# Attention with look-ahead scores and a gated feed-forward: heads taken in pairs, 64-row products in three passes, weights read transposed

## The reference

```python
xn = layernorm(x)                                  # x: 8 x 512 x 256
qu, ku, vu, qc, kc, vc = split(xn @ W_qkv.T)       # 8 heads of 64 each
term1     = where(causal, 0, (qc * s) @ vu.T)      # 512 x 512 per head
lookahead = where(causal, sigmoid((qu * s) @ ku.T), 0)
Su        = term1 @ lookahead.T
scores    = (qc * s) @ kc.T - silu(Su)
attn      = softmax(where(causal, -max, scores)) @ vc
h         = silu(xn @ w_gate.T) * (xn @ w_up.T)    # hidden 768, int weights / 127
out       = x + attn @ W_out.T + h @ w_down.T
```

## Time and profile before

| | |
|---|---|
| median of 3 runs | 1201.95 us |
| profiled execution, first to last instruction | 1197.5 us |
| PE, PEld busy | 1155.7 us (97%), 1049.7 us (88%) |
| DVE, ACT, POOL busy | 1046.0 us (87%), 924.4 us (77%), 543.8 us (45%) |
| prologue and first projections | to about 27 us |
| attention | about 27 to 1003 us |
| feed-forward and sum | 1003 to 1197.5 us |

### The profile page before, as it was taken

The page is one execution under the profiler, slowest core; times in us unless marked ns, Lnnn a source line. Parts: engine busy times, 40 slices in busy tenths (PEclk is TensorE's granted clock), DMA queues, the critical chain, the costliest instruction groups (busy, mean ns, idle before and its releaser), DMA issues. The chain is left out here.

```text
span 1197.5 us, 25023 instructions
## 1 busy us (share of the span) xinstructions
PE 1155.7 (97%) x7324; PEld 1049.7 (88%) x7324; DVE 1046.0 (87%) x2421; ACT 924.4 (77%) x2074; POOL 543.8 (45%) x915
## 2 busy tenths in 40 slices
PE   6999999999999999999999999999999987999997
PEld 5899898989898989898989898989899976999997
DVE  6799889989998999899989998999889987878885
ACT  5788888888888888888888888888888864434443
POOL 0455555546555555555655565556555550000000
PEclk9999999999999999999999999999999998999999
DMA  5111211121112111211121112111321112243332
GB/s 172 40 45 45 63 45 45 45 63 44 44 44 63 44 44 44 63 44 44 44 63 44 44 44 63 44 44 44 101 59 45 45 54 79 89 140 102 108 109 67
DMA packets 41491, 74.16 MB, mean 62 GB/s; under 512 B 3504, under 2 KB 24496, under 8 KB 41392
## 3 DMA queue, kind: packets, MB, share of 16 engines
q1 hardware_dynamic: 41392, 73.15, 21.2%
HBM read 27.00 MB, written 12.58 MB: 33 GB/s over the span
## 5 line engine op out<-in xcount | busy, mean ns | idle before, releaser
L719 PE MATMUL Su<-L_s,T_s 128*128 128x128 f32 (+3 forms) x1920 | 292.5, 299 | 1.8 <-POOL T_s L543 1.8
L719 PEld LDWEIGHTS Su<-L_s,T_s 128*128 128x128 f32 x1920 | 279.3, 190 | 16.4 <-POOL T_s L543 2.7
L553 POOL TENSOR_SCALAR prob<-prob,inv 128x512 f32<-128x512 f32 x252 | 274.5, 1096 | 13.1 <-DVE inv L1134 12.9
L638 PE MATMUL X<-xT,W 128*128 128x512 f32 x960 | 242.5, 394 | 3.0 <-PEq L130 3.0
L638 PEld LDWEIGHTS X<-xT,W 128*128 128x128 f32 x960 | 172.7, 189 | 33.6 <-issue 3.2
L527 POOL TENSOR_SCALAR_AFFINE_SELECT gate<-gate 128x128 f32<-128x128 f32 (+1 forms) x192 | 66.3, 346 | 262.3 <-DVE gate L1111 197.3
L899 ACT ACTIVATE gate<-Su 128x512 f32<-128x512 f32 (+1 forms) x192 | 101.4, 528 | 71.5 <-PE Su L719 70.4
L907 ACT ACTIVATE prob<-prob,least 128x512 f32<-128x512 f32 (+3 forms) x256 | 142.4, 561 | 7.6 <-DVE least L1122 7.2
L1111 DVE SCALAR_TENSOR_TENSOR gate<-gate,Su 128x512 f32<-128x512 f32 (+1 forms) x192 | 114.2, 595 | 27.3 <-ACT gate L899 17.4
L543 POOL TENSOR_SCALAR_AFFINE_SELECT T_s<-T_s 128x256 fp32r<-128x256 f32 x256 | 131.1, 542 | 13.3 <-DVE T_s L1103 9.2
L535 POOL TENSOR_SCALAR_AFFINE_SELECT tanh_l<-tanh_l 128x128 f32<-128x128 f32 (+1 forms) x192 | 62.6, 333 | 160.0 <-ACT tanh_l L875 157.8
(11 more groups left out here) (85 smaller groups left out, 2132.7 us busy)
## 6 DMA issues: line engine op xcount, KB each, us to landing
qu_s<-qu_s SPq DMA_DIRECT2D x64, 256.0 KB, 3.7
qc_s<-qc_s SPq DMA_DIRECT2D x64, 256.0 KB, 3.5
xb<-in_L_attn_x SPq DMA_DIRECT2D x16, 512.0 KB, 4.6
heads_out<-o_s SPq DMA_DIRECT2D x32, 256.0 KB, 2.0
f_o_in<-heads_out SPq DMA_DIRECT2D x8, 1024.0 KB, 5.7
f_xres<-in_L_attn_x SPq DMA_DIRECT2D x8, 512.0 KB, 4.6
out<-f_y SPq DMA_DIRECT2D x8, 512.0 KB, 3.2
w_raw<-in_L_attn_W_qkv SPq DMA_DIRECT2D x6, 512.0 KB, 7.4
```

Source lines behind the costliest of these rows:

```text
L553: last = pool.tensor_scalar(v, v, inv[:, hp, w - 1:w], None, ALU.mult)
L638: last = pe.matmul(bank[:, :], sh.W[:, a, k, cols], xT[:, c, k, :], start=(n == 0), stop=(n == 3 * KD - 1))
L719: last = pe.matmul(Su[slot][:, at:at + (J + 1) * P], T_s[:, hp, a, to:to + P], L_s[:, hp, c, WIDE[J + 1]:WIDE[J + 1] + (J + 1) * P], start ...
```

## The change

Attention now takes a pair of heads in a step, 32 steps instead of 64. The two heads' 64 numbers lie in partitions 0 to 63 and 64 to 127, as the projection leaves them; no operand is stored twice and SP's `dup` is gone. L, T and Sc are made in three passes (`PRODUCTS`) of 64-row matmuls, one for each head in turn, into two neighbouring banks. ACT, DVE and POOL then treat both heads in one instruction of 2 x 512 or 2 x 256 columns, except `minus_scores`, exp, reciprocal and `norm`, which stay single because each has a number per row and head. The eight banks are handed round by a table (`TURNS`), and every group of products waits for the groups that held its banks (`BEFORE`, `take_bank`). The tile that tanh writes is now the softmax's own (`tanh_l = prob`), so `minus_scores` of a pair waits until the next pair's look-ahead has been split. The order of a step is the new `step` of each engine. The weights come in transposed, so that the prologue's and the end's transposes of weights fall away, and a weight is split 1024 or 1536 columns at a time.

```diff
@@ prologue, build
-            for n in range(groups):
-                ...
-                for i in range(per):
-                    last = pe.transpose(banks[n % 6][:, i * P:(i + 1) * P],
-                                        raw[:, per * t + i, k * P:(k + 1) * P], sh.ident[:, :])
+                sp.dma_start(raw[:, :, t * INNER:(t + 1) * INNER],
+                             W_qkv[:, t * INNER:(t + 1) * INNER].rearrange("(k p) c -> p k c", p=P)) \
+                act.wait_ge(loaded[t], 16)
+                act.activation(sh.W[:, HIGH, :, cols], raw[:, :, cols], ACT.Copy,
-        a = np.ascontiguousarray(inputs[name])
+        a = np.ascontiguousarray(a if a.ndim == 3 else a.T)
@@ attention: banks
-X_BANKS = 4
+TURNS = [("L", 0, (0, 1)), ("L", 1, (2, 3)), ("L", 2, (4, 5)), ("T", 0, (6, 7)), ("T", 1, (0, 1)), ("T", 2, (2, 3)),
+         ("O", 0, (4, 5)), ("proj", QU, (6,)), ("proj", KU, (7,)), ("proj", VU, (0,)), ("V", 0, (1,)),
+         ("Sc", 0, (2, 3)), ("Sc", 1, (4, 5)), ("Sc", 2, (6, 7)), ("proj", QC, (0,)), ("proj", KC, (1,)),
+         ("XT", 0, (2, 3)), ("Su", 0, (4, 5)), ("Su", 1, (6, 7)), ("PT", 0, (0, 1)), ("PT", 1, (2,)),
+         ("PT", 2, (4, 5)), ("Su", 2, (6, 7))]
+        tanh_l = prob
@@ attention: products (the same in term1 and scores)
-                    for a in (HIGH, LOW):
-                        last = pe.matmul(bank[:, at:at + w * P], ku_s[:, s % 2, J * P:(J + 1) * P],
-                                         qu_s[:, s % 2, a, 0:w * P], start=(a == 0), stop=(a == 1))
+                    for n, (a, c) in enumerate(PRODUCTS):
+                        for h in range(2):
+                            rows = slice(h * DH, (h + 1) * DH)
+                            last = pe.matmul(both[:, h, at:at + w * P], ku_s[rows, a, J * P:(J + 1) * P],
+                                             qu_s[rows, c, 0:w * P], start=(n == 0), stop=(n == 2))
@@ attention: the order of PE
+            def step(part, b, q, g, back1, back2, ahead):
+                for j in range(3):
+                    look_ahead(part, b, g, j)
+                for j in range(3):
+                    term1(part, b, q, g, j)
+                if back2:
+                    attend(part, b, q, g)
+                if ahead:
+                    project(part, b, q, g, QU)
+                    project(part, b, q, g, KU)
+                    project(part, b, q, g, VU)
+                    values_into(take_bank(part, b, g, "V", 0), (q + 1) // 2 % 2, (q + 1) % 2)
+                if back1:
+                    for j in range(3):
+                        scores(part, b, q, g, j)
+                if ahead:
+                    project(part, b, q, g, QC)
+                    project(part, b, q, g, KC)
+                if q == 2:
+                    transpose_x(part, b, g)
+                sum_up(part, b, g, 0)
+                sum_up(part, b, g, 1)
+                if back1:
+                    turn_probs(part, b, g)
+                sum_up(part, b, g, 2)
@@ attention: ACT
-                act.activation(tanh_l[:, c:c + n], bank[:, 0:n], ACT.Tanh, scale=LOOK_SCALE).then_inc(tanh_done, 1)
+                act.activation(tanh_l[:, :, c:c + n], bank("L", j)[:, :, 0:n], ACT.Tanh, scale=LOOK_SCALE) \
+                   .then_inc(tanh_done, 1)
-                for h in range(2):
-                    last = act.activation(dst, bank[rows, :], ACT.Copy)
+                act.activation(dst, bank("proj", t)[:, :], ACT.Copy).then_inc(proj_high, 1)
@@ attention: DVE, the middle of a step
+                if back2:
+                    sum_o(g - 2, q % 2)
+                if ahead:
+                    low_proj(g + 1, QU, par)
+                    low_proj(g + 1, KU, par)
+                    low_proj(g + 1, VU, par)
+                    low_values(g + 2, (q + 1) // 2 % 2, (q + 1) % 2)
+                if back1:
+                    minus_scores(g - 1, 0)
+                    minus_scores(g - 1, 1)
+                    inverse(g - 1, 0)
+                    minus_scores(g - 1, 2)
@@ attention: SP
-                sp.dma_start(words[DH:P, 0, :, :], words[0:DH, 0, :, :]).then_inc(done, 16)
-                sp.dma_start(words[0:DH, 1, :, :], words[DH:P, 1, :, :]).then_inc(done, 16)
```

More of the change, by code:

```diff
@@ L699, in term1 @@
-                last.then_inc(filled, 1)
-            def scores(g, s, j):
-                hp, par, slot = s % 2, (s // 2) % 2, (s + j) % 2
-                if not (isinstance(g, int) and 3 * g + j < 2):
-                    pe.wait_ge(scores_emptied, 3 * g + j - 1)
+                    for n, (a, c) in enumerate(PRODUCTS):
+                        for h in range(2):
+                            rows = slice(h * DH, (h + 1) * DH)
+                            last = pe.matmul(both[:, h, at:at + w * P], vu_s[rows, a, J * P:(J + 1) * P],
+                                             qc_s[rows, q % 2, c, J * P:SEQ], start=(n == 0), stop=(n == 2))
@@ L831, in _ @@
-            for t in FIRST_PAIR:
-                project(FIRST, 0, -2, t, 0)
-            values(FIRST, 0, -2)
-            batches(pe, program)
-            finish(BATCH - 1)
+                    for n, (a, c) in enumerate(PRODUCTS):
+                        for h in range(2):
+                            rows = slice(h * DH, (h + 1) * DH)
+                            last = pe.matmul(both[:, h, at:at + w * P], qc_s[rows, par, a, I * P:(I + 1) * P],
+                                             kc_s[rows, par, c, 0:w * P], start=(n == 0), stop=(n == 2))
@@ new lines, in attend @@
+            def attend(part, b, q, g):
+                both = take_bank(part, b, g, "O", 0)
+                for h in range(2):
+                    slot = (2 * (q - 2) + h) % HEADS
+                    pe.wait_ge(PT_low, after(g - 2, 1 + h))
+                    for K in range(TT):
+                        at = WIDE[TT - K]
+                        for c in (HIGH, LOW):
+                            last = pe.matmul(both[:, h, K * P:SEQ], v_s[:, slot // 4, K, slot % 4, :, :],
+                                             PT_s[:, h, c, at:at + (TT - K) * P],
+                                             start=(K == 0 and c == HIGH), stop=(K == TT - 1 and c == LOW))
+                    last.then_inc(o_filled, 1)
@@ new lines, in _ @@
+            for t in PROJ_ORDER:
+                if t == QC:
+                    pe.wait_ge(proj_low, proj_count(0, VU))
+                if t == KC:
+                    pe.wait_ge(v_low, 1)
+                project_into(bank("proj", t)[:, :], t, 0)
+                if t == VU:
+                    values_into(bank("V", 0), 0, 0)
+            batches(pe, lambda b, part: run_steps(b, part, step))
+            attend(LAST, BATCH, 0, LAST_G + 1)
+            for j in range(3):
+                scores(LAST, BATCH, 0, LAST_G + 1, j)
@@ L917, in copy_o_low @@
[L917 to L935 removed]
+                    act.wait_ge(scores_emptied, after(g - 1, j))
@@ new lines, in gate_of, with exp_of @@
+                act.wait_ge(Su_filled, after(g, j))
+                act.activation(gate[:, :, c:c + n], bank("Su", j)[:, :, 0:n], ACT.Tanh, scale=SU_SCALE) \
+                   .then_inc(gate_done, 1)
+            def exp_of(g, j):
+                act.wait_ge(scores_emptied, after(g, j))
+                for h in range(2):
+                    for w in ROWS[j]:
+                        v = prob[:, h, WIDE[w]:WIDE[w] + w * P]
+                        last = act.activation(v, v, ACT.Exp, bias=least[:, h, w - 1:w], scale=-1.0,
+                                              accum_out=total[:, h, w - 1:w])
+                last.then_inc(exp_done, 1)
```

1236 lines of the change are left out of this document (451 added, 785 removed).

## The result

The kernel with the change takes **1366.9 us** (median of 4 runs, 1361.7 to 1368.6), where the kernel before took 1201.6 in the same rounds (1200.6 to 1202.2). The ratio is 1.137, interval 1.135 to 1.139. The forecast was 1274, range 1235 to 1345: the direction was right, but the loss is 165 us and not 72, and the time lies above the range.

The account below looks back on a forecast made before the run. It took PE's work to bound the kernel before, and a serial chain of 32.1 us a step after. Attention 47 us late plus 25 at the end gave 1270 us span, 1274 us with 4.5 for the median; range 1235 to 1345.

Parts of the forecast that it names:

- The ring: In each step, hand-overs through all engines from L's start to the next L; T at 4.9, scalings over at 28.6 us.
- the sum of a step: In attention, the serial chain of one step, L to next L, was put at 32.1 us, 2.1 more than before.
- PE's clock falls: Rival: a half-clock stretch follows each stall before T, 1.5 us x 30 steps = 45, giving 1319 us; chance 0.15.
- Su needs L and T split, which DVE has done near 12.6: Within a step, DVE's splits of L and T were to end 12.6 us after L starts, delaying nothing.
- The two ends: Before and after attention's middle: x first transposed at 102.7 us, 13 early; last transposes to feed-forward 74 us, 25 more.
- The estimate: At attention's end, the last pair was put at 35 us, 14 of them PT, its split, O, sum and store.
- The set of 64-row products: On PE, one pair's 64-row matmuls for L, T or Sc were put at 2.35 us, midway between 2.03 and 2.7.
- The bound of 2.7: On PE, a set takes 2.7 us if two half weight loads need 0.22 us one after the other.
- The halves take turns: Rival: the two heads' 64-row matmuls don't run together, a set is 4.05 us, the kernel 1364 us; chance 0.10.
- A switch drains PE: Rival: changing between 64 and 128 rows drains PE, at least 0.15 us each, +0.3 a step, 1283 us; chance 0.12.
- PE stays the bound: Rival: results come before PE asks, a step is PE's 27.6 to 28.5 us, the kernel 1147 or 1173; chance 0.08.
- the forecast's sum: PE's own work for a pair in attention was to become 28.5 us, 1.1 us less than before.

Follow-up runs that it names:

- edit 1: Against the changed kernel, ACT makes the gate of Su's third group ahead of the three tanh of L instead of behind them: 1266.4 us, ratio 1.056.
- 5: Against the changed kernel, ACT's gate goes ahead of L's tanh and POOL's masks of T wait for DVE's split of L: 1233.6 us, ratio 1.027.
- 6: On the kernel with gate first and masks late, DVE instead of POOL scales the middle group of four probabilities: 1201.9 us, ratio 1.001.
- Edit 2: Against the changed kernel, one wait more on POOL holds its masks of T until DVE has split L: 1346.7 us, ratio 1.123.
- Edit 8: On the kernel with gate first, masks late and DVE scaling, PE's batch loop turns before a batch's last PT, behind 48 queued matmuls: 1187.2 us, ratio 0.989.
- experiment 7: Against the changed kernel, both heads' L, T and Sc read partitions 0 to 63, so head 1's own are left out: 1620.9 us, one run.

## Why the forecast had the direction right and the size wrong

**The ring was right.** Of its steps, from L's start in the step at 540.23:

| | forecast | measured | from |
|---|---|---|---|
| T starts | 4.9 | 4.8 | 545.01 |
| values made | 15.3 | 15.2 | 555.40 |
| `minus_scores` begins | 16.7 | 17.4 | 557.66 |
| first scaling | 19.9 | 20.8 | 560.98 |
| scalings over, PT starts | 28.6 | 29.5 | 569.73 |

The times of `minus_scores` and of the first scaling come from DVE's and POOL's timelines of the kernel after:

```profile
553.84 1.39 DVE L911 TENSOR_TENSOR o_s<-X,o_low 64x512 f32<-64x512 f32 x2
...
557.66 0.68 DVE L879 CUSTOM_DVE_ANT_0 prob<-X,gate 128x512 f32<-128x512 f32 x1
```

```profile
560.98 8.52 POOL L457 TENSOR_SCALAR prob<-prob,inv 128x512 f32<-128x512 f32 x8 [7.61 <-DVE inv L891]
```

That this ring, and not PE, set the time is shown and not only read: edits 1, 5 and 6 each shorten one member of it, and take 100, 33 and 32 us off.

**The step that failed is the sum of a step, 32.1 us for 34.75.** 28 x 2.65 = 74 of the 93 us that were missed. It has three parts.

- *The clock, some 1.1 to 1.4 us.* "PE's clock falls" stood as a rival at 0.15 with 1.5 us a step. Its mechanism was right: T and O are 1.5 us longer in the step from 506.41 than in the next, and edit 1 took 1.5 us of busy time off PE beyond the stall. Its chance was wrong. The one argument against it was that PE is busy on both sides of the stall, and that held nothing up. It should have been a term of the chain. In the step from 506.41 it costs less than its 1.5: the values come 1.5 later than in the step at 540.23, but PT starts only 0.7 later (30.2 for 29.5), since at full clock the ring waits for DVE's queue there. In others it costs more: the step from 576.14, just behind a turn, takes 37.2 us, and in it T takes 3.89 us, O 3.95 and PT 4.07. The 1.1 to 1.4 are what is left once the other two parts are taken off; that is a difference, not a measurement.
- *DVE beside POOL, 1.0 us.* The ring at full clock is 29.5 + 2.15 + 1.5 = 33.2 us with PT and Su's last group, 1.1 over the forecast. "Su needs L and T split, which DVE has done near 12.6": it has them done at 553.84, 13.6 after L's start, and the O sum and the projections' low parts queue behind. The splits were priced by the earlier trace rows, where widths were scaled and neighbours were not. Edit 2 shows the neighbour's share.
- *The loop's turn, 0.2 to 0.5.* In the kernel after L starts at 438.28, 472.39, 506.41, 540.23 and 576.14: three steps of 33.8 to 34.1, and one of 35.9 at the turn. Of the 28 steps five hold a turn, 35.8 us in the mean, and the others 34.5. How much of that is the turn and how much the clock behind it no run separates: at 569.73 PT runs slowly too (3.75 us), in the turn before, at 432.51, it does not (2.40) and L waits 2.04. Edit 8 gave back 0.5 a pair. The forecast had no term for it.

**The two ends, +10 us each.** x was first turned at 112.5 where 102.7 was forecast. L of step 0 starts at 29.59 instead of 26.3: the first 18 projections take 5.93 us behind an idle PE, where they take 4.31 later on, and L waits 1.50 us for DVE's low parts with nothing else to do for PE. The first two steps are longer by the rest.

```profile
17.65 5.93 PE L513 MATMUL X<-xT,W 128*128 128x512 f32 x18 [6.55 <-PEq L126]
...
29.59 2.19 PE L543 MATMUL X<-qu_s,ku_s 64*128 64x512 f32 x24 [1.50 <-DVE kc_s L816]
```

From the last transposes of x to the feed-forward it was 84, not 74. The chain of the last pairs, beside the earlier trace rows:

```profile
1117.37 9.95 PE L588 MATMUL X<-L_s,T_s 128*128 128x512 f32 x48 [1.17 <-DVE least L879]
...
1136.84 4.47 PE L624 MATMUL X<-PT_s,v_s 128*128 128x512 f32 x16 [5.50 <-DVE PT_s L902]
...
1152.96 4.53 PE L597 MATMUL X<-ident,prob 128*128 128x128 f32 x20 [5.75 <-DVE prob L925]
1159.86 3.97 PE L624 MATMUL X<-PT_s,v_s 128*128 128x512 f32 x16 [2.37 <-DVE PT_s L902]
1170.05 2.06 PE L1124 MATMUL f_G<-xT,W 128*128 128x512 f32 x4 [6.22 <-issue]
```

PE waits 1.2 to 6.2 us ahead of each of these, and all but the last then run slowly: PT takes 4.5 us here and 2.4 in the middle, O 4.5 and 2.8, Su's first two groups 9.95 and 7.06. The estimate priced PE's part at full clock, at which they would be 8 us shorter ((9.95 - 7.06) + (4.47 - 2.77) + (4.53 - 2.40) + (3.97 - 2.77)). 74 + 10 + 10 makes 94, the miss.

**The set of 64-row products: 2.12 us, not 2.35.** The error is in the good direction, 0.4 us a step on the chain. The bound of 2.7 rested on two half loads that need 0.22 one after the other. The loads start 3 ns apart, as the matmuls do. By the Trainium skill, "TensorE: Matmul & The Clock Gate", section "Measured speedup vs the span model", the estimate was near 2.03, and the trace is closer to that page than to my middle.

**The other rivals.** *The halves take turns* gives 1364, and the kernel took 1366.9. It is refuted all the same: a set of 2.12 us, and the experiment with one half at 4.03. A time that fits says nothing about its cause. *A switch drains PE*: where no switch lies, a run ends 0.16 us after the next has started (547.12 + 2.77 against 549.73); at the switches, 64 to 128 rows and back, 0.07 after (545.01 + 2.18 against 547.12, 553.88 + 1.59 against 555.40). A switch thus costs 0.09 us, and the starts, which are not modelled as the ends are, say the same: 0.21 us from the last matmul of the values to the first of Sc, 0.12 from one matmul of the values to the next. For the switches out of a set this is inside the 2.12. The Trainium skill, "TensorEngine Tiling (Array Packing)", section "Key Properties", says that changing the tiling mode drains TensorE; the trace has a price for it, and four of them are under 0.4 us a step. *PE stays the bound*: that is what edit 8 comes near, 28.9 a pair, once both waits and most of the turn are gone; that kernel still has the longer end, 78.3 us from the last transposes of x to the feed-forward against 47.5.

**The prices of the edits.** The three that answer the ring (1, 5 and 6) add no work to PE: their gains are the ring's members, and the change loses by its order and not by its 64-row products. With that order mended a pair takes 28.88 us, 1.1 less than before. That is the figure of the forecast's sum, but by luck: with the set as measured the sum says 1.7, and what the turns of the loop still cost takes the difference. The kernel is 14 us faster than before.

## What to carry to other kernels

When heads or tiles are merged into one step, draw the ring of hand-overs through all engines before counting what each saves. A kernel whose steps overlap three ways hides hand-overs that a merged step puts in a row, and less work on every engine can make it slower. A stall of PE of a few microseconds that comes in every step is to be priced twice, as time and as the clock that falls behind it, even where PE is busy on both sides of it. Take the duration of an instruction from a row in which its new neighbour runs beside it, or put a range on it.

## What the runs showed of the hardware

- 64-row matmuls of the two halves run at once whether they alternate in the program or stand in blocks of three: 2.12 us a set against 4.03 from one half, starts 3 and 10 ns apart.
- With one half alone (experiment 7) the granted clock is 0.858 over the kernel, against 0.933, though T's waits are shorter there (2.1 us a step for 2.5), and it stays low longer, 0.54 over 18.5 us. Two waits close to each other (2.35 us ahead of L at the loop's turn, 1.9 ahead of T) are not needed for it: in the next step one wait of 2.15 us is followed by 12 us at 0.50. That the half array is the reason is likely; it rests on one run.
- At a switch between 64 and 128 rows PE loses 0.09 us.
- DVE's scalar_tensor_tensor and POOL's affine_select, both from and to SBUF, slow each other: 684 to 1118 ns for 512 columns of the one, 637 to 1620 for 512 of the other. DVE's split of T, which reads PSUM too, ran beside the same masks with no loss on either side: 1223 ns, and 640.
- PE loses 1.9 to 2.5 us where a loop turns, even with matmuls queued ahead of the jump. What sets it stays open, as does why it is 1.9 ahead of PT and 2.5 ahead of L.
